# Two bias vectors of an attention block's setup as one-column products, and new lists for the setup

## What is computed

```python
n = layernorm(x)
x1 = layernorm(n, ln1_g, ln1_b); x2 = layernorm(ctx, ln2_g, ln2_b)
q = x1 @ Wq + bq; k = x2 @ Wk + bk; v = x2 @ Wv + bv
x = x + softmax(q @ k.T * E**-0.5) @ v @ Wo + bo
y = layernorm(x)
h = y @ (w_fc, ternary, scaled).T + gate * (y @ v.T @ fast_b.T @ u.T)
x = x + relu(h)**2 @ (w_proj, ternary, scaled).T
```

## Time and profile before

| | us |
|---|---|
| median of three runs | 780.16 |
| the profiled execution, whole | 780.34 |
| its span | 778.5 |
| TensorE busy in the span | 767.4 |
| VectorE busy | 549.3 |
| ScalarE busy | 368.7 |
| GpSimd busy | 107.6 |

### The profile page before, as it was taken

One profiled execution on the slowest core, in us unless ns is written; L12 is line 12 of the kernel. 1 busy time (PEld: TensorE's weight loads), 2 busy tenths in 40 slices (PEclk: granted clock), 3 DMA queues, 4 the chain that ended last, 5 costly groups with the idle time before them and its releaser, 6 DMA issues.

```text
span 778.5 us, 10613 instructions
## 1 busy us (share of the span) xinstructions
PE 767.4 (99%) x3775; PEld 638.8 (82%) x3775; DVE 549.3 (71%) x1120; ACT 368.7 (47%) x690; POOL 107.6 (14%) x125
## 2 busy tenths in 40 slices
PE   7999999999999999999999999999999999999998
PEld 4578788888888888888888888888888888888886
DVE  5999766778676777667766786768667686656435
ACT  4998644354425535354434544254442644233332
POOL 3101310200311030110312020210202002000001
PEclk9999999999999999999999999999999999999999
DMA  8743331163115322063214422063212530030101
GB/s 304 259 141 119 61 90 41 18 98 89 55 42 79 60 69 91 10 100 69 81 42 62 65 77 96 1 99 61 99 41 40 75 90 1 1 54 2 53 0 55
DMA packets 180125, 56.20 MB, mean 72 GB/s; under 512 B 167620, under 2 KB 167894, under 8 KB 180072
## 3 DMA queue, kind: packets, MB, share of 16 engines
q1 hardware_dynamic: 149940, 50.79, 26.6%
q10 hardware_dynamic: 30132, 4.73, 3.7%
HBM read 26.92 MB, written 8.39 MB: 45 GB/s over the span
## 4 chain that ended last, share of the span: by engine, by line
PE 97%; DVE 1%; ACT 1%; DMA 0%; issue 0%; ACTq 0%; DVEq 0%
PE H L1362 30%; PE O L1343 29%; PE G L1224 26%; PE H L1368 4%; PE H L1224 1%; PE H L1201 1%; PE H L1208 1%; PE G L1308 1%; PE O L1417 1%; PE O L1383 1%; DMA vrows<-in_L_xattn_bv_dram 0%; PE G L1252 0%; PE H L1189 0%; DVE x2a L1057 0%; PE H L1194 0%
## 5 line engine op out<-in xcount | busy, mean ns | idle before, releaser
L1343 PE MATMUL O<-projT,qbuf 128*128 128x512 f32 x992 | 242.1, 390 | 0.0
L1343 PEld LDWEIGHTS O<-projT,qbuf 128*128 128x128 f32 x992 | 185.0, 188 | 38.2
L780 ACT ACTIVATE rbuf<-H,scf 128x512 f32<-128x512 f32 x128 | 87.5, 684 | 125.1 <-DVE qbuf L1116 74.1
L1362 PE MATMUL H<-even_group,fcT 128*128 128x512 f32 x512 | 127.5, 391 | 0.0
L1362 PE MATMUL H<-odd_group,fcT 128*128 128x512 f32 x512 | 127.3, 391 | 0.0
L1112 DVE TENSOR_TENSOR rbuf<-rbuf 128x512 f32<-128x512 f32 x128 | 91.5, 723 | 45.9 <-ACT rbuf L780 45.9
L788 ACT ACTIVATE qbuf<-rbuf 128x512 fp32r<-128x512 f32 x125 | 78.5, 628 | 89.4 <-PE O L1343 62.3
L1116 DVE TENSOR_TENSOR qbuf<-rbuf,qbuf 128x512 fp32r<-128x512 f32 x125 | 85.9, 688 | 36.8 <-ACT qbuf L788 36.2
L1362 PEld LDWEIGHTS H<-odd_group,fcT 128*128 128x128 f32 x512 | 95.3, 188 | 19.3
L1362 PEld LDWEIGHTS H<-even_group,fcT 128*128 128x128 f32 x512 | 95.1, 188 | 19.2
L1224 PE MATMUL G<-Wvo,tT 128*128 128x512 f32 x270 | 64.7, 389 | 0.0
(11 more groups left out here) (201 smaller groups left out, 993.7 us busy)
## 6 DMA issues: line engine op xcount, KB each, us to landing
xb<-in_x_dram SPq DMA_DIRECT2D x8, 1024.0 KB, 4.9
n_blocks<-n_rows SPq DMA_DIRECT2D x112, 64.0 KB, 2.3
ctxb<-in_ctx_dram SPq DMA_DIRECT2D x8, 768.0 KB, 4.4
n_blocks<-ctxb SPq DMA_DIRECT2D x112, 48.0 KB, 2.2
wring<-in_L_ffn_w_fc_dram SPq DMA_DIRECT2D x16, 256.0 KB, 6.7
wring<-in_L_ffn_w_proj_dram SPq DMA_DIRECT2D x16, 256.0 KB, 2.8
out_dram<-x2a SPq DMA_DIRECT2D x8, 512.0 KB, 2.7
x_blocks<-x_rows SPq DMA_DIRECT2D x56, 64.0 KB, 3.5
```

The costliest lines, as they stand in the source:

```text
L780: nc.scalar.activation(rbuf[:, j % 2, :], banks[f"H{j % 2}"][:, :], ACT.Relu, scale=scf[:, j:j + 1]).then_inc(relu_made, 1)
L1343: mm = pe.matmul(banks[f"O{t}"][:, :], qbuf[:, j % 2, h, t * P:(t + 1) * P], projT[:, j, :], start=(j == 0 and h == HI), stop=(j == ends a ...
L1362: pe.matmul(banks[f"H{j % 2}"][:, :], fcT[:, k, j * P:(j + 1) * P], xnT[:, h, k, :], start=(k == 0 and h == HI), stop=False)
```

## The change

The products that spread g2, the step `g2` and the multiplication by `g2row` go. In their place ScalarE multiplies each block of Wk's rows by its column of g2 in SBUF (`wks:0` to `2`) before TensorE turns it; the turned blocks are then plain copies, of which ScalarE makes one and VectorE two. `bqacc` accumulates in the row of bq itself. Job `bq` becomes four products of one column each: the partial sums are the weights, and a column of ones is what moves. Its result is a column for each 128 features, `bqc`. The new job `tb` multiplies the turned, scaled Wk by these columns: 12 products of one column, accumulated in fours. VectorE copies the three sums to `tbias`. GpSimd and ScalarE have no part in it. As `x2a` isn't used by this any more, Wo is loaded from SP's queue, behind `ring:7`. SP loads all of Wq and Wk ahead of the ring. The lists of all engines are laid anew, and two of the four PSUM banks of the first group's attention change places.

```diff
     if n >= 8:
-        return ("G0", "H0", "G1", "H1")[n % 4]
+        return ("G0", "H1", "G1", "H0")[n % 4]
...
     "sp": (
-        "Wq:0 Wq:1 ring:0 Wq:2 bqrow ring:1 bo Wq:3 ring:2 Wk:2 ring:3 Wk:0 Wk:1 x:0 ring:4 ring:5 ring:6 "
-        "ring:7 Wv:0 ring:8 ring:9 ctx:0 ring:10 ring:11 ring:12 ring:13 ring:14 ring:15 lowrank ring:16 ring:17 ring:18 "
+        "Wq:0 Wq:1 Wq:2 bo Wk:0 Wq:3 Wk:1 Wk:2 ring:0 ring:1 bqrow ring:2 ring:3 x:0 ring:4 ring:5 ring:6 Wv:0 ring:7 "
+        "Wo ring:8 ring:9 ctx:0 ring:10 ring:11 ring:12 ring:13 ring:14 ring:15 ring:16 lowrank ring:17 ring:18 "
...
     "pe": (
-        "wqT:0 wqT:1 vecs wqT:2 wqT:3 bq:0 wkT:0 wkT:1 wkT:2 M:0 M:1 turn:0 turn:1 wvT:0 turn:2 turn:3 n1T:0 wvT:1 "
-        "M:2 turn:4 wvT:2 turn:5 turn:6 n1T:1 wvo:0 n1T:2 wvo:1 n1T:3 wvo:2 turn:7 turn:8 n2T:0 turn:9 turn:10 n2T:1 "
-        "turn:11 turn:12 co:0 n2T:2 M:3 n2T:3 fb:0 turn:13 turn:14 turn:15 t:0 t:1 t:2 turn:16 turn:17 turn:18 "
...
+        "wqT:0 wqT:1 vecs wqT:2 wqT:3 wkT:0 wkT:1 wkT:2 M:0 M:1 bq:0 M:2 turn:0 n1T:0 turn:1 tb:0 turn:2 wvT:0 turn:3 "
+        "wvT:1 turn:4 n1T:1 wvT:2 turn:5 wvo:0 turn:6 n1T:2 wvo:1 turn:7 n1T:3 wvo:2 turn:8 turn:9 n2T:0 n2T:1 "
+        "turn:10 turn:11 co:0 n2T:2 M:3 n2T:3 turn:12 turn:13 fb:0 turn:14 turn:15 t:0 t:1 t:2 turn:16 turn:17 "
...
     "act": (
-        "wqT:0 vecs wqT:2 abs:0 abs:1 wqT:3 g2 abs:2 tb Wo abs:4 abs:5 M:0 abs:6 M:1 nx0 wvT:0 store:0 store:1 nx1 "
-        "wvT:1 abs:8 store:2 M:2 n1T:0 abs:9 n1T:1 nx2 store:3 store:4 abs:10 wvT:2 store:5 wvo:0 nx3 abs:12 n1T:2 "
-        "nc0 abs:13 wvo:1 n1T:3 nc1 abs:14 store:6 abs:16 wvo:2 store:7 store:8 n2T:0 n2T:1 nc2 abs:17 abs:18 nc3 "
...
+        "wqT:0 vecs wks:0 wqT:2 wks:1 wks:2 wkT:1 abs:0 abs:1 M:0 abs:2 abs:4 abs:5 abs:6 M:1 abs:7 nx0 nx1 M:2 "
+        "store:0 store:1 store:2 n1T:0 wvT:0 wvT:1 abs:8 wvT:2 store:3 nx2 nx3 n1T:1 store:4 store:5 abs:9 store:6 "
+        "abs:10 abs:12 wvo:0 abs:13 n1T:2 wvo:1 nc0 abs:14 abs:15 n1T:3 nc1 abs:16 wvo:2 store:7 n2T:0 store:8 n2T:1 "
...
     "dve": (
-        "wqT:1 bqacc abs:3 bq:0 wkT:0 wkT:1 invert:0 wkT:2 xs01 xs23 abs:7 round:0 round:1 M:0 round:2 round:3 "
-        "invert:1 M:1 round:4 round:5 round:6 coacc M:2 round:7 cs01 n1T:0 n1T:1 cs23 abs:11 abs:15 invert:2 round:8 "
-        "wvo:0 round:9 n1T:2 round:10 n1T:3 round:11 wvo:1 invert:3 round:12 wvo:2 n2T:0 round:13 n2T:1 co:0 round:14 "
...
+        "wqT:1 wqT:3 wkT:0 wkT:2 bqacc xs01 xs23 M:0 M:1 abs:3 invert:0 round:0 bq:0 round:1 round:2 round:3 invert:1 "
+        "M:2 tb:0 round:4 round:5 round:6 coacc n1T:0 abs:11 cs01 cs23 round:7 n1T:1 invert:2 wvo:0 round:8 wvo:1 "
+        "n1T:2 round:9 n1T:3 invert:3 round:10 round:11 wvo:2 n2T:0 n2T:1 round:12 round:13 co:0 abs:19 round:14 "
...
+                elif kind == "Wo":
+                    sp.dma_start(Wo_s[:, :, :], Wo.rearrange("(c p) e -> p c e", p=P)).then_inc(wo_in, 16)
...
-                    elif st == "tb":
-
-                        pool.wait_ge(job_dve, job_count(JOBS.index(("bq", 0)), "dve"))
-                        for m in range(KC):
-                            pool.wait_ge(wk_in[m], 16)
-                            nc.gpsimd.tensor_tensor(x2a[:, m, :], Wk_s[:, m, :], x2a[:, KC, :], ALU.mult
-                                                    ).then_inc(tb_products, 1)
...
                 elif kind == "t":
                     if b < 0 and t == 0:
-                        act.wait_ge(tb_made, KC)
+                        job_read(act, JOBS.index(("tb", 0)))
                     nc.scalar.activation(tT[:, HI, t, :], bank[:, :], ACT.Identity, bias=tbias[:, t:t + 1]
...
-                    elif kind == "tb":
-
-                        act.wait_ge(vcols_made, 1)
-                        for m in range(KC):
-                            act.wait_ge(tb_products, m + 1)
-                            nc.scalar.activation(x2a[:, m, :], x2a[:, m, :], ACT.Copy, scale=g2c[:, m:m + 1],
-                                                 accum_out=tbias[:, m:m + 1]).then_inc(tb_made, 1)
-                    elif kind == "Wo":
-                        act.wait_ge(tb_made, KC)
-                        act.dma_start(Wo_s[:, :, :], Wo.rearrange("(c p) e -> p c e", p=P)).then_inc(wo_in, 16)
...
-                    elif kind == "g2":
-                        act.wait_ge(g2_full, 1)
-                        nc.scalar.activation(g2row, banks["G0"][:, 0:DC], ACT.Copy).then_inc(g2_made, 1)
+                    elif kind == "wks":
+                        act.wait_ge(vcols_made, 1)
+                        act.wait_ge(wk_in[j], 16)
+                        nc.scalar.activation(Wk_s[:, j, :], Wk_s[:, j, :], ACT.Copy, scale=g2c[:, j:j + 1]
+                                             ).then_inc(wk_scaled, 1)
...
-                    gains = g2row[:, c * P:(c + 1) * P].unsqueeze(1).broadcast_to([P, KE, P])
-                    nc.vector.tensor_tensor(WkT[:, :, c * P:(c + 1) * P], wide, gains, ALU.mult).then_inc(job_dve, 1)
+                    nc.vector.tensor_copy(WkT[:, :, c * P:(c + 1) * P], wide).then_inc(job_dve, 1)
                 elif kind == "wvT":
                     nc.vector.tensor_copy(WvT[:, :, c * P:(c + 1) * P], wide).then_inc(job_dve, 1)
                 elif kind == "bq":
-                    nc.vector.tensor_copy(x2a[:, KC, :], bank[:, :]).then_inc(job_dve, 1)
+                    nc.vector.tensor_copy(bqc[:, :], bank[:, 0:KE]).then_inc(job_dve, 1)
+                elif kind == "tb":
+                    nc.vector.tensor_copy(tbias[:, :], bank[:, 0:KC]).then_inc(job_dve, 1)
...
-                        acc = x2a[:, 0, :]
+                        acc = bqrow
...
                     elif kind == "wkT":
-                        pe.wait_ge(wk_in[c], 16)
+                        pe.wait_ge(wk_scaled, c + 1)
...
                     pe.wait_ge(bq_summed, 1)
-                    mm = pe.matmul(bank[:, :], ones[:, :], x2a[:, 0, :], start=True, stop=True)
+                    for k in range(KE):
+                        mm = pe.matmul(bank[:, k:k + 1], bqrow[:, k * P:(k + 1) * P], ones[:, 0:1], start=True, stop=True)
+                elif kind == "tb":
+
+                    job_read(pe, JOBS.index(("bq", 0)))
+                    for m in range(KC):
+                        for k in range(KE):
+                            mm = pe.matmul(bank[:, m:m + 1], WkT[:, k, m * P:(m + 1) * P], bqc[:, k:k + 1],
+                                           start=(k == 0), stop=(k == KE - 1))
                 elif kind == "M":
...
-                        for k in range(KC):
-                            row = 2 * KD + k
-                            mm = pe.matmul(banks["G0"][:, k * P:(k + 1) * P], ident[0:NV, row:row + 1].broadcast_to([NV, P]),
-                                           vrows[:, :], start=True, stop=True)
-                        mm.then_inc(g2_full, 1)
```

22 lines of the change are left out of this document (8 added, 14 removed), and 26 rows, old and new, of the table PROLOGUE.

## The result

| us | before | after |
|---|---|---|
| median of four runs | 780.19 (779.97 to 780.77) | 789.18 (788.96 to 789.33) |
| profiled execution, whole | 780.34 | 788.96 |
| span | 778.5 | 787.1 |

The changed kernel is slower by 9.0 us in the medians: ratio 1.0109, 95% interval 1.0092 to 1.0126. Forecast were 782.7 us and a range that ended at 785.0. The direction was right; the forecast size, 2.5 us, was little more than a fourth of what came.

The account below looks back on a forecast made before the run. TensorE, busy 99% of the span, was taken as the bound. The terms -2.8 + 0.4 + 3.6 + 1.2 + 0.7 - 0.3 - 0.3 gave +2.5 us, so 782.7 us, with an 8 in 10 range of 780.0 to 785.0.

Parts of the forecast that it names:

- The early start: At start-up, with Wq and Wk loaded first, M:0 starts at 12.3 us instead of 15.06: -2.8 us.
- bq and tb pass at 0.112 us: The added one-column float32 products on TensorE take 32 passes, paced by the weight load: +3.6 us.
- The wait ahead of bq: TensorE waits after M:1 until VectorE has read its half of M:0: +1.2 us, bounds 0 and 1.9.
- n1T:0's wait: In the setup, TensorE's wait ahead of n1T:0 goes because its tile now comes early enough: -0.3 us.
- the terms up to the scores: The setup's forecast terms, said to put the first score product at about 59.4 us instead of 56.83.
- "+0.4 us" for the clock: At M:0's start, the first 0.8 us run at 1.2 GHz if the clock rises when it did: +0.4 us.
- the rival of the late clock: Clock rises only when M:0 and M:1 are through: +3.6 us on the forecast, 786.3 us; chance 0.1.
- a rise half-way: Late-clock case with the rise at 17 us: the wait ahead of bq hides all but 0.5 us.
- The wait behind tb: ScalarE and VectorE stand some 2 us during tb and pass it on to wvo:2 and co: +0.7 us.
- The loop from there on as before: After the first score product, the TensorE-bound loop over the groups is untouched and only moves with the setup.
- "-0.3 us" for one rounding less: Between the scores and the first L, VectorE has one rounding less to do: -0.3 us.
- nothing for the ring: In the setup's loads, Wo behind ring:7 lands at about 21.8 us, ahead of first use; no cost counted.

Follow-up runs that it names:

- e5: Changed kernel with piece 2's turning ahead of tb, VectorE's roundings 4 to 6 ahead of its copy of tb, and ScalarE's sum of piece 8 earlier; 786.87 us.
- e6: Changed kernel with three of tb's four accumulated products left out, 3 one-column products instead of 12; 786.25 us.
- e2: Kernel before the change with its 512-column bias product cut to one column; 782.37 us.
- e9: Changed kernel with ScalarE's list end as before, the next group's last normalization ahead of storing piece 25, and turn:31 and round:31 put back; 785.62 us.
- e13: e5 with ScalarE's sums of pieces 9 and 10 ahead of three stores, and VectorE's inversion and rounding of piece 8 earlier; 785.99 us.
- e17: e5 with tb's 12 one-column products done four times over, 96 passes instead of 24; 803.30 us.
- e16: Kernel before the change with four unused 128-column products on TensorE ahead of Wq's arrival; 780.17 us.
- e10: e5 with the loads of the low-rank weights issued ahead of ring:16 instead of behind it; 788.39 us.
- e15: Changed kernel with three unused products in TensorE's start, the list orders of e5, e9 and e13, and M:0 and M:1 read out earlier; 785.29 us.
- e7: Changed kernel with ScalarE's list end as before and the next group's last normalization ahead of storing piece 25; 787.90 us.

## Why the prediction was wrong

*Direction, and the terms on TensorE: right.* The early start gave -2.4 in the profile and -2.8 in e5 (forecast -2.8). bq and tb pass at 0.112 us, 32 passes, +3.6 as said; e6 confirms it by 18 passes. The Trainium skill, "TensorE: Matmul & The Clock Gate", section "LDWEIGHTS", has a load cost by its columns and not by its rows; the trace agrees, with 0.112 us a pass for weights of 128 rows as for those of 16. It doesn't agree with the floor of 25 ns in "Back-to-back issue gap" of the same page. The wait ahead of bq was 1.1 us in e5 (forecast 1.2); in the profile of after the slow M:0 hid it, as the rival said, and a wait of 0.94 us ahead of M:2, which I hadn't listed, stood in its place. n1T:0's wait went. One sum was off: the terms up to the scores add up to 59.6 us for the first score product, not 59.4. It came at 63.51.

*The step that failed most is "+0.4 us" for the clock, "if the clock rises when it did".* It rose behind 17.3 us, after seven passes of M: 2.3 us instead of 0.4. That was the rival of the late clock, to which I gave 0.1. I had written that of a rise half-way, at 17 us, "the wait ahead of bq hides all but 0.5 us". By the prediction's own paces it would be 0.8, and against e5 it was 1.0 us at bq and 2.0 at M:2, since the late end of M:1 made its own half late and so M:2 wait. I took the time of one rise in one profile for a property of the start. The rows show it anywhere from before 12.2 to behind 17.3 us for the same steps, and e2 shows what the wide product was worth: taking 511 of its columns away made before slower.

*The wait behind tb, "+0.7 us", passed on by VectorE and ScalarE.* Both did stand idle 2.2 us, as forecast, but that was not passed on: with the stand cut to 0.2 us in e6 the way from Wvo to co stays at 14.7 us. The 0.9 us more than before have other reasons: 0.5 is the longer wait ahead of co, for the readout of Wvo's last block, and 0.2 a wait ahead of Wvo's third block that stands in e6 as well. So that the number came out near is luck.

*"The loop from there on as before".* It was not looked at. The diff moves turn:31 by one place and ScalarE's last steps by some; e9 gives the 1.85 us back. The prediction costed steps that were moved only in the first 46 us.

*"-0.3 us" for one rounding less between the scores and L, and nothing for the ring.* In their place stand 0.0 and 1.6 us (1.12 + 0.51). e13 gives 1.2 of these back: from co to the scores it takes 16.44 us, after 17.67, before 16.04. A late scale and a rounding behind a readout had made later pieces late.

By the parts, against the forecast 2.5: M:0 0.4 us less early, clock +1.9, 0.94 of wait ahead of M:2 for 1.2 ahead of bq -0.3, up to co +0.2, ring and steps up to the scores +1.6, +0.3 for a gain that didn't come, entry of the loop +1.85. That is 8.6 in the profile; it was 9.0 in the medians. A range for such a change needs the late clock at its full price and a term for every list that changes.

## What to carry over

Before an early start is booked as a gain, see what stands at TensorE's clock rise and whether the step that moves ahead of it is the first long one: its passes cost double there, and the same steps had their rise 5 us apart in different runs. One-column products are priced by their weight load, 0.112 us a pass and two passes each in float32, and by what they do to the clock. And where all lists are laid anew, compare the last dozen steps of each list as closely as the first: one turning, one tile earlier, put GpSimd's adds on top of VectorE's critical instructions and cost 1.3 us, a third of what the new products did.

## What was not expected of the hardware

- A TensorE that is busy by the profile from 29.0 to 39.7 us with nothing but one-column products holds a granted clock of 0.50 (e17).
- The same steps have their rise of the clock anywhere from before 12.2 us to behind 17.3, and products ahead of Wq's arrival didn't bring it forward (12.9 us in e16, one profile), while with 512-column products in later gaps it came by 7.7 to 9.9 us (five profiles).
- In nine of twenty profiles the granted clock fell to 0.50 within the first 70 us, and stayed there for 3.4 to 13.7 us. Some falls came behind an idle time of under 2 us (1.94 in e10, 1.62 in e15, none over 0.65 in e6). What makes one come is not shown, but for the stretch of one-column products.
- The granted clock column reads 1.00 ahead of the first rise; only the distance of the starts tells the level there.
- With GpSimd adding two tiles from SBUF, VectorE's two-input instructions take 1.0 to 1.8 us instead of 0.69 (e7), and transpositions stay at 0.70.
